# Off-diagonal blur products of a two-level pyramid issued as two 64-row tiles on TensorE

## The chip, the cores and the metric

One core of a Trainium2 chip runs the whole program once. The metric is the device time of that execution in microseconds. Beside it there is one profiled execution, whose trace is read below.

## What is computed

The reference adds four blocks in sequence to an input of 16 images, 64 channels and 16x16 pixels. Each block begins with a group norm. The change touches the second block, which needs a small blur pyramid of the normalised input:

```python
G = x; pyr = [x]
for i in range(2):
    G = depthwise_gauss(G, gauss2d(2*i + 3, 1.6 * 2**(i/3)))   # 3x3, then 5x5, zero padded
    pyr.append(G)
for i in (1, 2):
    L = pyr[i-1] - pyr[i]
    A = softmax(L, over pixels) @ L.T                           # 64x64 for each image
    att = att + softmax(A)
```

The other parts of this block (keys, queries, values, the attention of the level 0) run around it. The pixels of an image are called tokens here: 256 tokens, row by row.

## The kernel before

All arithmetic is fp32, and each fp32 matmul stands in the trace as two instructions. Images go in pairs, two images times 64 channels on the 128 partitions: 8 tiles `t` of 128 by 256, in two groups `g` of four, and in four pairs of tiles `j`. A hand-written order of steps, the list `SCHEDULE`, is walked by every engine, each doing its own share of each step. Around the change it reads: `add` (DVE: end of block 1), `pyramid` of group 0, `norm` 1 of group 1, `levels` 0, `in1` 0, `levels` 1, `in1` 1, `levels_T` 0, `pyramid` of group 1, `levels_T` 1, then `levels` of group 1 between the `scores1` of group 0. So PE issues the second group's mean product (`group_means`, L376) right behind the first pyramid, and the whole norm of group 1 waits for it: DVE L887 to L889, GpSimd's power L1587, DVE L897, and L905, which writes the normalised tiles.

A blur of a token-major tile is a product with a 256 by 256 matrix: `lap1` and `lap2` hold identity minus blur 1, and blur 1 minus blur 2. The input `xT` has the tokens on the partitions, in two chunks `k` of 128 tokens (NK = 2). For each level `s` and output chunk `jn`, `pyramid` claims a PSUM bank and accumulates two full 128x128 by 128x512 products, `k` = 0 and 1. ACT copies each bank to SBUF as `lT` (L1428, `pyramid_out`). The blur matrices are banded: an output token depends on tokens at most three image rows, 48 tokens and a few, away. So of the product with the other chunk only the 64 tokens next to the border between the chunks have weights that are not zero.

`claim` takes the next bank of a ring of six, and puts a wait on PE for the engine that last read that bank:

```python
n = ring[kind][claimed[kind] % len(ring[kind])]
if n in reader: pe.wait_ge(*reader[n])
reader[n] = (sem_of_reader, value)
```

The banks that the second pyramid takes are, six claims back, those of `xT`, keys, queries and values of the fourth pair (`in1` 1 of group 1). The bank of the keys is read last by ACT's exponentials of the keys, L1400 (`exp_keys`), which count `ek_ready`; L1400 itself waits for DVE's L1074. The queries' and values' banks are read by DVE L1093. In `in1`, ACT also does L1405 (copies of transposed banks), L1420 (exponentials of the levels) and L1434 (exponentials of the queries). Transposes on PE are L518, L554 (`level_back`), L565 (`exp_T`), L574 and L609; L521 and L528 are the projections; L589 are the channel products. After the second pyramid, DVE's L1085 (row maxima of a level) waits for L554.

Other places of the kernel already use parts of the array: `y2` (L457) runs two 64-row by 128-column tiles into two banks, `keys_values3` (L716, L718) four 64 by 64 tiles, next to full products (L658 ahead, L705 behind).

Of the kernel before, what the change touches and what calls it, by code (L numbers as in the profile page):

```python
# [27 lines left out]
NK = HW // P  # L28
# [104 lines left out]
def program(nc, x_in, const_in, weight_in, param_in, out):  # L133
# [11 lines left out]
    with ExitStack() as ctx:  # L145
# [8 lines left out]
        def bank(n, a=0, b=512):  # L154
            return psum[:, n * 512 + a:n * 512 + b]
# [8 lines left out]
        def cst(name):  # L164
            return const[:, const_at[name][0]:const_at[name][1]]
# [9 lines left out]
        lap = [None, cst("lap1").rearrange("p (k n) -> p k n", k=NK), cst("lap2").rearrange("p (k n) -> p k n", k=NK)]  # L175
# [56 lines left out]
        def tokens_of_pairs():  # L232
            return pairs(HW, "p (k t c) -> p k t c", 2, k=NK)
# [19 lines left out]
        xT = tokens_of_pairs()  # L253
        lT = [xT] + [tokens_of_pairs() for _ in range(2)]
# [98 lines left out]
        def claim(pe, key, sem_of_reader, value, kind="bulk"):  # L353

            n = ring[kind][claimed[kind] % len(ring[kind])]
            claimed[kind] += 1
            if n in reader:
                pe.wait_ge(*reader[n])
            reader[n] = (sem_of_reader, value)
            where[key] = n  # L360
            return n
# [5 lines left out]
        def _(pe):  # L367
            mm, tr = nc.tensor.matmul, nc.tensor.transpose
# [163 lines left out]
            def pyramid(g):  # L532

                pe.wait_ge(xT_ready, 2 * g + 2)
                for s in (1, 2):
                    for jn in range(NK):
                        step = (g * 2 + s - 1) * NK + jn
                        n = claim(pe, ("lT", step), lT_ready, step + 1)
                        for k in range(NK):
                            last = mm(bank(n), lap[s][:, k, jn * 128:(jn + 1) * 128],  # L540
                                      xT[:, k, 4 * g:4 * g + 4, :].rearrange("p t c -> p (t c)"),
                                      start=(k == 0), stop=(k == NK - 1))
                        last.then_inc(lT_mm, 1)

            def level_back(j, s):

# [257 lines left out]
            def start3():  # L804
# [3 lines left out]
            steps = {"norm": group_means, "ctx": context, "gate": gates, "taps": tap_sums, "conv": shift_taps,  # L808
                     "y1": y1, "y2": y2, "y3": y3, "mlp1": channel_mlp1,
                     "mlp2": channel_mlp2, "h4T": tokens4, "conv7": conv7, "add": add0, "in1": in1, "pyramid": pyramid,  # L810
                     "levels": levels1, "levels_T": levels_T, "scores1": scores1, "mix": mix1, "out1": out1, "own": own_rows,
                     "residual": residual, "parts": tap_parts, "sums": sums, "start3": start3}
# [7 lines left out]
            for w in range(NT + STEPS_MORE):  # L820
                t, r = divmod(w, 4)
# [1036 lines left out]
```

## Time and profile before

| | |
|---|---|
| median of 3 runs | 274.06 us (273.55 to 275.35) |
| profiled execution | 272.08 us |
| its span, first to last instruction | 270.3 us |
| PE, DVE, ACT, POOL busy | 79%, 68%, 50%, 13% |
| both pyramids (L540) on PE | 14.2 us, 32 instructions |

PE is the matrix engine, PEld its weight loads, which run beside it. DVE is VectorE, ACT ScalarE, POOL GpSimd. In a timeline a row gives the start, the time, engine, line, operation, and in brackets how long the engine had been idle and who released it. Instructions of one line that follow each other are merged into one row. A matmul's own time is longer than the distance to the next one, as they are pipelined: the distance between starts is what a stream pays.

### The profile page before, as it was taken

What the parts mean: (1) busy time and instruction counts of PE and PEld (TensorE: products, weight loads), DVE (VectorE), ACT (ScalarE), POOL (GpSimd) and SP (SyncE); (2) the same over time, 40 slices, a digit from 0 to 9 for tenths busy, and PEclk for the clock granted to TensorE, in tenths of its full rate; (3) what the DMA queues carried; (4) which work ended last, traced back from release to release, by engine and by line L of the source; (5) the groups of instructions that cost most, each with busy time, mean ns of one, the idle gap of its engine ahead of it and who ended that gap; (6) DMA issues with size and microseconds to landing.
All of it is one profiled execution on the core that took longest, in us unless ns stands there. A gap on an engine that the chain in (4) does not pass through costs nothing. (4 is left out here: it accounts for less than half of the span.)

```text
span 270.3 us, 6261 instructions
## 1 busy us (share of the span) xinstructions
PE 214.1 (79%) x2402; PEld 129.9 (48%) x2402; DVE 185.1 (68%) x521; ACT 136.2 (50%) x338; POOL 35.5 (13%) x64
## 2 busy tenths in 40 slices
PE   0376898755499877989589599699789959998974
PEld 0344674423375565677454133345544634464552
DVE  2464533457689599198877647865968597779892
ACT  1025268823255367889554233774367455634510
POOL 1833000000100100000010467203320010000000
PEclk9999799998599999999999999999979999999995
DMA  6930000000000000000000045351034004400001
GB/s 183 407 140 2 1 0 4 0 2 0 0 0 0 4 0 0 0 4 2 2 4 2 24 118 145 76 132 41 6 84 105 10 0 114 125 19 22 4 19 58
DMA packets 8685, 12.57 MB, mean 46 GB/s; under 512 B 1616, under 2 KB 7888, under 8 KB 8400
## 3 DMA queue, kind: packets, MB, share of 16 engines
q1 hardware_dynamic: 8048, 11.37, 14.5%
q10 hardware_dynamic: 608, 0.80, 1.0%
q8 instruction: 19, 0.31, 0.5%
q14 instruction: 10, 0.08, 0.1%
HBM read 4.93 MB, written 1.05 MB: 22 GB/s over the span
## 5 line engine op out<-in xcount | busy, mean ns | idle before, releaser
L1512 ACT ACTIVATE region<-psum 128x512 f32<-128x512 f32 x32 | 19.0, 594 | 22.3 <-PE psum L767 22.1
L1506 ACT ACTIVATE region<-region 128x512 f32<-128x512 f32 x32 | 20.1, 628 | 19.3 <-DVE region L1246 19.1
L1239 DVE TENSOR_REDUCE smax<-psum 128x8 f32<-128x512 f32 x32 | 21.9, 684 | 8.3 <-PE psum L757 8.1
L1587 POOL TENSOR_TENSOR small<-small 128x4 f32<-128x4 f32 x8 | 8.2, 1023 | 146.6 <-DVE small L889 146.6
L739 PE MATMUL psum<-region,w 128*32 128x512 f32 x160 | 21.8, 616 | 2.2 <-ACT v_pad L1491 2.1
L767 PEld LDWEIGHTS psum<-const,region 128*128 128x128 f32 x128 | 14.2, 144 | 17.7 <-ACT region L1506 9.0
L1246 DVE TENSOR_TENSOR region<-psum,smax 128x512 f32<-128x512 f32 x32 | 22.0, 687 | 0.6
L767 PE MATMUL psum<-const,region 128*128 128x128 f32 x128 | 21.0, 287 | 1.6 <-ACT region L1512 1.6
L785 PE MATMUL psum<-region 128*64 128x18 f32 x512 | 20.5, 213 | 0.7 <-ACT region L1512 0.7
L785 PEld LDWEIGHTS psum<-region 128*64 128x64 f32 x512 | 17.5, 137 | 6.1 <-issue 5.2
L376 PE MATMUL psum<-small,const 128*128 128x8 f32 x16 | 3.6, 296 | 15.2 <-DVE small L878 15.2
L1405 ACT ACTIVATE region<-psum 128x512 f32<-128x512 f32 x20 | 11.0, 623 | 8.8 <-PE psum L518 8.8
L540 PE MATMUL psum<-region,const 128*128 128x512 f32 x32 | 14.2, 597 | 0.0
L871 DVE BATCH_NORM_STATS2 small<-X 128x6 f32<-128x256 f32 x32 | 12.3, 419 | 2.8 <-ACT X L1376 1.4
L1233 DVE SCALAR_TENSOR_TENSOR xn_pad<-v_pad,small,xn_pad 128x256 f32<-128x256 f32 x32 | 13.8, 476 | 0.0
L376 PEld LDWEIGHTS psum<-small,const 128*128 128x128 f32 x16 | 3.0, 232 | 19.8 <-DVE small L878 18.4
L1444 ACT ACTIVATE region<-psum,small 128x64 f32<-128x64 f32 x24 | 9.4, 425 | 5.7 <-DVE small L1125 5.7
L757 PE MATMUL psum<-region 32*64 32x256 f32 x256 | 9.9, 418 | 1.8 <-DVE region L1246 1.2
L1531 ACT ACTIVATE region<-psum 128x512 f32<-128x512 f32 x12 | 6.2, 609 | 9.2 <-PE psum L669 9.2
L1635 POOL COPY region<-v_pad 128x256 f32<-128x256 f32 x16 | 5.8, 404 | 37.8 <-ACT v_pad L1491 37.8
L411 PE MATMUL psum<-region 128*32 128x256 f32 x96 | 8.6, 508 | 2.3 <-issue 2.3
L528 PEld LDWEIGHTS psum<-weight,region 128*128 128x128 f32 x64 | 8.3, 204 | 4.2 <-ACT region L1405 2.2
(180 smaller groups left out, 472.6 us busy)
## 6 DMA issues: line engine op xcount, KB each, us to landing
region<-v_pad SPq DMA_DIRECT2D x60, 80.0 KB, 2.1
weight<-weight_in SPq DMA_DIRECT2D x1, 1600.0 KB, 12.8
const<-const_in SPq DMA_DIRECT2D x1, 1170.0 KB, 9.6
X<-x SPq DMA_DIRECT2D x4, 256.0 KB, 5.4
out<-xn_pad SPq DMA_DIRECT2D x8, 128.0 KB, 1.7
weight<-weight_in SPq DMA_DIRECT2D x1, 918.0 KB, 6.8
region<-xn_pad SPq DMA_DIRECT2D x6, 76.5 KB, 2.4
region<-xn_pad ACTq DMA_DIRECT2D x6, 76.5 KB, 2.5
```

Source lines behind the costliest of these rows:

```text
L540: last = mm(bank(n), lap[s][:, k, jn * 128:(jn + 1) * 128], xT[:, k, 4 * g:4 * g + 4, :].rearrange("p t c -> p (t c)"), start=(k == 0), st ...
L739: last = mm(bank(n)[32 * c:32 * c + 32, :], w4[:, c % 2, dx, :], v4[:, j % 2, c, :, :, dx:dx + W], start=(dx == 0), stop=(dx == 4), tile_p ...
L757: last = mm(bank(banks[r], a2 * 256, a2 * 256 + 256)[64 * c:64 * c + 64, :], q3[rows, j % 2, a, :], km[rows, j % 2, a, :, :].rearrange("p ...
L767: last = tr(bank(n, q * 128, (q + 1) * 128), e3[:, w % NE, q * 128:(q + 1) * 128], ident)
L785: last = mm(dst[half, a2, 1 - b, h:h + 2, :].rearrange("p h e -> p (h e)"), e3T[:, w % NE, at + 64 * c:at + 64 * c + 64], va[:, 4 * t + 2 ...
L871: v.bn_stats(stats[l][:, t, :], X[:, t, :]).then_inc(dve_small, 1)
L1233: v.scalar_tensor_tensor(out=a, in0=win, scalar=pe_w[:, 5 * PE_ROWS + i:5 * PE_ROWS + i + 1], in1=prev, op0=ALU.mult, op1=ALU.add).then_in ...
L1239: v.tensor_reduce(smax[:, w, :], src, X_AXIS, ALU.max).then_inc(smax_ready, 1)
L1246: v.tensor_tensor(s_sub[:, w % NE, :].rearrange("p (h m) -> p h m", h=HEADS), src, smax[:, w, :].unsqueeze(2).broadcast_to([P, HEADS, AP_] ...
L1405: a.activation(dst[:, :, 2 * j:2 * j + 2, :].rearrange("p k t c -> p t k c"), bank(where[(*key, step)]).rearrange("p (t k c) -> p t k c", ...
L1506: a.activation(e3[:, u % NE, :], s_sub[:, u % NE, :], ACT.Exp, scale=HD ** -0.5).then_inc(e3_ready, 1)
L1512: a.activation(e3T[:, u % NE, :], bank(where[("e3T", u)]), ACT.Copy).then_inc(e3T_ready, 1)
```

## The change

In each level both banks are claimed first. Then come the two diagonal products (output chunk `jn` with input chunk `jn`) with all 128 rows, and then the two off-diagonal ones over 64 rows only: for `jn` = 0 partitions 0 to 63 of chunk 1, for `jn` = 1 partitions 64 to 127 of chunk 0. They have different row positions in the array and different banks.

```diff
                 pe.wait_ge(xT_ready, 2 * g + 2)
                 for s in (1, 2):
+                    steps_of = [(g * 2 + s - 1) * NK + jn for jn in range(NK)]
+                    banks = [claim(pe, ("lT", step), lT_ready, step + 1) for step in steps_of]
                     for jn in range(NK):
-                        step = (g * 2 + s - 1) * NK + jn
-                        n = claim(pe, ("lT", step), lT_ready, step + 1)
-                        for k in range(NK):
-                            last = mm(bank(n), lap[s][:, k, jn * 128:(jn + 1) * 128],
-                                      xT[:, k, 4 * g:4 * g + 4, :].rearrange("p t c -> p (t c)"),
-                                      start=(k == 0), stop=(k == NK - 1))
-                        last.then_inc(lT_mm, 1)
+                        mm(bank(banks[jn]), lap[s][:, jn, jn * 128:(jn + 1) * 128],
+                           xT[:, jn, 4 * g:4 * g + 4, :].rearrange("p t c -> p (t c)"), start=True, stop=False)
+                    for jn in range(NK):
+                        near = slice(64 * jn, 64 * jn + 64)
+                        mm(bank(banks[jn]), lap[s][near, 1 - jn, jn * 128:(jn + 1) * 128],
+                           xT[near, 1 - jn, 4 * g:4 * g + 4, :].rearrange("p t c -> p (t c)"), start=False, stop=True,
+                           tile_position=(64 * jn, 0)).then_inc(lT_mm, 1)
```

The other engines' steps and all waits on `lT_mm` are as before.

## Rows read from the trace of the kernel before

**Rows 1.** Timeline, PE: both pyramids, and what stands behind them

```profile
81.61 1.99 PE L436 MATMUL psum<-region,const 8*128 8x256 f32 x8
83.53 7.13 PE L540 MATMUL psum<-region,const 128*128 128x512 f32 x16
90.50 0.28 PE L376 MATMUL psum<-small,const 128*128 128x8 f32 x2
...
105.76 7.11 PE L540 MATMUL psum<-region,const 128*128 128x512 f32 x16
112.71 1.47 PE L565 MATMUL psum<-const,region 128*128 128x128 f32 x12
...
115.33 0.60 PE L609 MATMUL psum<-const,region 128*128 128x128 f32 x4
```

**Rows 2.** Timeline, DVE: the norm of group 1, and behind the second pyramid

```profile
88.66 0.36 DVE L878 BATCH_NORM_AGGREGATE small<-small 128x2 f32<-128x6 f32 x4
90.82 0.16 DVE L887 TENSOR_TENSOR small<-small,psum 128x4 f32<-128x4 f32 x1 [1.81 <-PE psum L376]
...
108.56 0.69 DVE L1104 TENSOR_TENSOR region<-region,small 128x512 f32<-128x512 f32 x1
115.10 0.69 DVE L1085 TENSOR_REDUCE small<-psum 128x2 f32<-128x512 f32 x1 [5.85 <-PE psum L554]
```

**Rows 3.** Busy time by stretch: engine, us (instructions), then the granted clock

```profile
92.70:109.25 16.55, 12.93 (x76) 9.30 (x77) 15.99 (x36) 10.57 (x37) 0.00 (x0) 1.00 0.00 0
98.10:102.87 4.77, 1.95 (x12) 1.13 (x11) 4.63 (x11) 3.28 (x11) 0.00 (x0) 1.00 0.00 0
109.25:115.10 5.85, 5.85 (x31) 3.85 (x30) 0.00 (x1) 5.25 (x11) 0.00 (x0) 1.00 0.00 0
```

**Rows 4.** Timeline, PEld: weight loads of the first pyramid, first and last

```profile
84.07 0.19 PEld L540 LDWEIGHTS psum<-region,const 128*128 128x128 f32 x1 [0.24 <-issue]
84.50 0.19 PEld L540 LDWEIGHTS psum<-region,const 128*128 128x128 f32 x1 [0.24 <-issue]
...
89.65 0.19 PEld L540 LDWEIGHTS psum<-region,const 128*128 128x128 f32 x1 [0.24 <-issue]
```

**Rows 5.** Timeline in short windows, PE: 64x128 tiles (L457), then full rows

```profile
39.35 0.49 PE L457 MATMUL psum<-region 64*128 64x256 f32 x2
...
39.67 0.60 PE L457 MATMUL psum<-region 64*128 64x256 f32 x4
...
39.88 0.60 PE L457 MATMUL psum<-region 64*128 64x256 f32 x4
...
40.10 0.38 PE L457 MATMUL psum<-region 64*128 64x256 f32 x2
40.41 0.40 PE L411 MATMUL psum<-region 128*32 128x256 f32 x1
```

**Rows 6.** Timeline in short windows, PE: full, 64x64 tiles, full

```profile
160.05 0.59 PE L658 MATMUL psum<-xn_pad,weight 128*128 128x512 f32 x1
160.57 0.64 PE L716 MATMUL psum<-region,weight 64*64 64x512 f32 x1
...
161.06 0.59 PE L716 MATMUL psum<-region,weight 64*64 64x512 f32 x1
...
161.59 0.70 PE L705 MATMUL psum<-region,weight 128*128 128x512 f32 x1
...
162.13 0.19 PEld L652 LDWEIGHTS psum<-X,const 128*128 128x128 f32 x1 [0.24 <-issue]
```

**Rows 7.** L540's own page: times of one, minimum, median, maximum

```profile
L540 PEld LDWEIGHTS psum<-region,const x32: 186/190/192, 83.5 to 111.9; 128*128 128x128 f32 x32
L540 PE MATMUL psum<-region,const x32: 590/592/697, 83.5 to 112.3; 128*128 128x512 f32 x32
```

**Rows 8.** Timeline, ACT, with the releases of DVE and PE it stands in

```profile
98.86 0.47 ACT L1400 ACTIVATE region<-psum,small 128x256 f32<-128x256 f32 x1
99.22 0.20 ACT L1400 ACTIVATION_READ_ACCUMULATOR region<-psum,small 128x1 f32 x1
...
106.45 0.47 ACT L1400 ACTIVATE region<-psum,small 128x256 f32<-128x256 f32 x1
106.81 0.20 ACT L1400 ACTIVATION_READ_ACCUMULATOR region<-psum,small 128x1 f32 x1
...
110.77 1.57 ACT L1428 ACTIVATE region<-psum 128x512 f32<-128x512 f32 x3
112.91 0.60 ACT L1428 ACTIVATE region<-psum 128x512 f32<-128x512 f32 x1 [0.56 <-PE psum L540]
113.41 2.06 ACT L1405 ACTIVATE region<-psum 128x512 f32<-128x512 f32 x4
116.03 0.47 ACT L1420 ACTIVATE region<-psum,small 128x256 f32<-128x256 f32 x1 [0.56 <-DVE small L1086]
```

**Rows 9.** Timeline, PE and PEld: a wait for L1400, here and in the second pyramid

```profile
99.56 0.63 PE L554 MATMUL psum<-const,region 128*128 128x128 f32 x4 [1.45 <-ACT region L1400]
...
107.13 0.19 PEld L540 LDWEIGHTS psum<-region,const 128*128 128x128 f32 x1 [0.24 <-ACT region L1400]
```

## The prediction

> **What bounds the kernel now.** I read the page's engine shares first and then, as they average over unlike stages, only the timelines of PE, DVE and ACT from the first pyramid to the scores. The first pyramid is 16 instructions from 83.53 to 90.50, with PE gap-free before it [rows 1]. Behind it in PE's queue is L376, whose inputs were ready when DVE ended its aggregate at 88.66 + 0.36 = 89.02; DVE then idled 1.81 us until L376 [rows 2]. So the first pyramid holds back the whole norm of group 1, by at most about 1.4 us: L376 could begin near 89.1 instead of 90.50. From 92.70 to 109.25 DVE is busy 15.99 of 16.55 us [rows 3]: everything there hangs on when DVE begins, and moves with it. The second pyramid starts at 105.76 and ends where L565 starts, 112.71 [rows 1]. DVE idles 5.85 us up to 115.10, PE is busy for the whole 5.85 us [rows 2, 3]: the second pyramid lies on the path outright. Later work waits on semaphores, with no clock time of its own, so I let a shift at 115 go through to the end at full size.
>
> **The products removed.** In a stream of full products the weight loads start 0.43 us apart (84.07, 84.50, ... 89.65: 5.58 us over 13 steps) and are hidden behind the matmuls [rows 4]. A pyramid is 16 such slots. The change turns 4 products of a level (8 instructions) into 2 full ones (4) and 2 of 64 rows (4). If the two of 64 rows run side by side they fill 2 slots. L457 shows this very shape with half the columns: two instructions start together at 39.35, two at 39.67, two at 39.88, two at 40.10 [rows 5], 0.215 us apart in the steady part, which is half of 0.43 for half of 512 columns. So 64-row tiles with different row positions and banks do overlap, pair by pair, first passes together and second passes together. A level goes from 8 to 6 slots, a pyramid from 16 to 12: 4 x 0.43 = 1.72 us less.
>
> **The changes of tile shape added.** Each level now goes from full to tiles and back. Where shapes change, the trace has gaps. Into tiles: L658 to L716 is 160.05 to 160.57, 0.52 instead of 0.43, so 0.09 [rows 6]; the first tile slot is 0.49 there (0.06 more, with a 64-column load of weights), and 0.32 instead of 0.215 for L457, so 0.10 more, with a 128-column load as here [rows 5]. Out of tiles: 0.53 from 161.06 to 161.59, so 0.10; 0.54 from 161.59 to the next weight load at 162.13, so 0.11 [rows 6]; L457 to L411 has 0.31 instead of 0.215, again 0.10 [rows 5]. I read it as a wait for the array and a load that is no longer hidden, and take c = 0.20 us for one change of shape, 0.19 in and 0.21 out, the nearest rows in shape. Two a level, 0.80 a pyramid; the last one out falls on L376 or L565. Bounds: 0 if these products see none of it; at most 0.35, if the array waits for a matmul's whole end (0.59 less 0.43) and the whole load of 0.19 is exposed [rows 7]. A pyramid is then shorter by 1.72 - 0.80 = 0.92 us.
>
> The Trainium skill (TensorEngine Tiling (Array Packing), Key Properties) says the same in general: changing the tiling mode, as against the tile, drains TensorE, and it names no price. It speaks against this change; the gaps of rows 5 and 6 agree with it. Going by that rule the sum keeps its 0.80; without it, it would be the rival of a free change below.
>
> **First pyramid.** Its four banks' former readers are all over by 83.5 (PE had no gap there), so the earlier claims cost nothing. It ends 0.92 us sooner, L376 starts at 89.58, above the 89.1 at which DVE would be late. DVE, POOL and all up to 105 move by 0.92. ACT copies both banks of level 2 back to back at the end instead of one; they are ready near 90.6, ahead of the transposes of level 2, the last step of a queue that had 0.91 us to spare in front of 93.5. Gain: 0.92 us.
>
> **The wait added in the second pyramid.** The second bank claimed is that of the keys of the last pair. Its reader is ACT L1400, whose last piece runs to 106.81 + 0.20 = 107.01 [rows 8]. Before, this bank was needed only after four slots, and the trace shows the weight load at 107.13 just behind that reader [rows 9]: it had fitted by a hair. Now PE waits for it ahead of the first product. What is queued behind it on PE is the whole pyramid, and behind that all of L565, L574, L554 for which DVE waits. An L1400 that ends at 99.22 + 0.20 = 99.42 lets a matmul start at 99.56 [rows 8, 9], 0.14 later. So the pyramid starts at 107.15 instead of 105.76: 1.39 us lost. Both times move together with DVE's chain, as L1400 waits for DVE's L1074, so the earlier gain does not shorten this. The banks of level 2 were read by DVE L1093, over by 107.1, and cost nothing.
>
> In the old time frame the second pyramid goes from 107.15 to 107.15 + 6.95 - 0.92 = 113.18, against 112.71: 0.47 later. L565 to L554 and DVE's L1085 come 0.47 later too. The cover to watch is ACT: both last copies (L1428) come together, so L1405 x4 starts about 1.06 later than 113.41 and ends its issue near 116.4; ACT's next, L1420, was held by DVE until 116.03 [rows 8], now 116.50. It just fits; if it did not, each tenth would count on the path.
>
> **The sum.** First pyramid -0.92, second -0.92, wait +1.39: -0.45 us. The profiled execution would go from 272.08 (span 270.3 and 1.8 around it) to 271.6; the median shown lies 2.0 above that execution, so 274.06 becomes 273.6 us.
>
> **Rivals.** In general, with c for one change of shape, the result is -(3.44 - 8c - 1.39) us.
>
> *Changes of shape are free* (c near 0). For it: in both places where I read gaps a semaphore wait stands on one of the instructions too, and it may be part of them. Against it: the gap shows at every border. The first pyramid gains only its limit of 1.4, the second 1.72 - 1.39 = 0.33: -1.7 us, 272.3. The Trainium skill (TensorE: Matmul & The Clock Gate, Measured speedup vs the span model) gives a packed group as one matmul and some 4 ns for each further tile, with no term for the border, and would end here.
>
> *The border and the wait outweigh the saved slots*: slower. One mechanism, PE time in the pyramids, decided at 8c = 2.05, c = 0.26. At the bound c = 0.35 it is +0.75, 274.8. For it: c is measured once for each direction and the load here has the full 128 columns. Against: no row has over 0.22.
>
> *The wait does not come*, as it would if L1400 were done before 105.8: -1.84, 272.2. Only against it: 107.01 is read directly, and it moves with what precedes the pyramid.
>
> *The tiles do not overlap* when they accumulate onto a full product's bank: no slot is saved, and the sum is 1.60 + 1.39 = +3.0, 277.1. L457 starts its accumulation in the tile, so this exact case is not in the trace; its overlap speaks against.
>
> *The clock falls* in the longer idle of PE. Against: from 98.10 to 102.87 PE is busy 1.95 of 4.77 us and the granted clock is 1.00 [rows 3]. At 1.2 GHz the second pyramid's 6 us could double at worst.
>
> **How the numbers follow.** The forecast has 0.53; free borders 0.13; outweighed 0.17; no wait 0.05; no overlap 0.04; clock 0.02; the rest, 0.06, lies on both sides. The forecast's own range, c from 0.15 to 0.25, is 273.2 to 274.0. The three runs of before span 1.8 us, so a median can lie most of 1 us off. The range goes from 272.0 (free borders, no wait) to 275.3 (c at its bound and half a us of scatter). A difference under 1%, 2.7 us, is about what a measurement of this kernel cannot tell from none. No rival that gains reaches it (the largest is 1.84), so faster has 0.04, from scatter; slower has the overlap, the clock and scatter on top of a larger c, 0.08.
>
> **What would show it.** In the profile after: the two 64-row instructions of a pass start within 0.01 us, and level by level slots of 0.43, then about 0.52, 0.53, 0.53, 0.54; L540 and its successors 12 slots and 6.05 us from start to successor; L376 near 89.6 and DVE idle near 0.9 before L887; PE idle about 1.4 before the second pyramid, put down to ACT L1400; DVE idle before L1085 about 6.3; the clock 1.00 throughout. A pyramid of 5.3 us means free borders; one above 6.35 us means that they outweigh; one above 7 that nothing overlaps; no gap before 105 means that I misread the bank ring.

## The result, and the profile after

The changed kernel takes 275.68 us (median of 20 runs, 273.63 to 281.02), the kernel before beside it 273.81 us (20 runs, 270.55 to 277.19). The medians are 1.87 us apart, 0.7%, where 0.45 us less was forecast, and 275.68 lies outside the stated range of 272.0 to 275.3. The ratio is 1.0097, 95% interval 1.0067 to 1.0127. The ratios, here and below, leave out executions more than 1.5% above the fastest of the same kernel, which are those above 274.6 us for the kernel before and those above 277.7 for the change, so they can overstate a loss that comes in some executions only. By either measure the change is slower, by 0.7 to 1%.

The pyramids themselves went nearly as forecast. PE's timeline after the change (start, time, engine, line):

```profile
79.83 1.99 PE L436 MATMUL psum<-region,const 8*128 8x256 f32 x8
81.75 1.98 PE L539 MATMUL psum<-region,const 128*128 128x512 f32 x4
83.67 1.13 PE L543 MATMUL psum<-region,const 64*128 64x512 f32 x4
84.72 1.98 PE L539 MATMUL psum<-region,const 128*128 128x512 f32 x4
86.64 1.13 PE L543 MATMUL psum<-region,const 64*128 64x512 f32 x4
87.70 0.39 PE L376 MATMUL psum<-small,const 128*128 128x8 f32 x2
...
104.44 1.96 PE L539 MATMUL psum<-region,const 128*128 128x512 f32 x4 [1.25 <-ACT region L1402]
106.33 1.13 PE L543 MATMUL psum<-region,const 64*128 64x512 f32 x4
107.39 1.99 PE L539 MATMUL psum<-region,const 128*128 128x512 f32 x4
109.31 1.13 PE L543 MATMUL psum<-region,const 64*128 64x512 f32 x4
110.36 1.53 PE L567 MATMUL psum<-const,region 128*128 128x128 f32 x12
...
128.28 1.08 PE L620 MATMUL psum<-region 64*64 64x256 f32 x8
```

L539 are the full products, L543 the tiles. The first pyramid takes 81.75 to 87.70, 5.95 us against 6.97 in [rows 1]. Four tile instructions take some 1.05 us up to the next full product, where two slots of 0.43 would be 0.86. PE (TensorE) now idles 1.25 us before the second pyramid, and the releaser is L1402, which is L1400 of before. That pyramid takes 5.92 us, against 6.95.

As the two executions differ ahead of the pyramids too, where the code is the same, I measure from an anchor: the start of the last L436 block before the first pyramid (81.61 in [rows 1], 79.83 here). To the start of the second block of out products of the first group (L618 before, at 130.56; L620 after, at 128.28) it is 48.95 us before and 48.45 after: 0.50 us gained. I call this the anchor distance, and that second block the anchor block. From there to the end of the span it is 270.3 - 130.56 = 139.7 before and 271.8 - 128.28 = 143.5 after: 3.8 us lost. And up to the anchor, where the two programs are the same, it was 1.78 us less. The sum, -1.78 - 0.50 + 3.82, is the +1.54 of the two spans.

DVE and ACT after, the rows that answer to [rows 2, 8]:

```profile
88.12 0.16 DVE L889 TENSOR_TENSOR small<-small,psum 128x4 f32<-128x4 f32 x1 [0.88 <-PE psum L376]
...
112.81 0.69 DVE L1087 TENSOR_REDUCE small<-psum 128x2 f32<-128x512 f32 x1 [6.26 <-PE psum L556]
```
```profile
110.46 1.09 ACT L1430 ACTIVATE region<-psum 128x512 f32<-128x512 f32 x2 [1.31 <-PE psum L543]
111.43 2.08 ACT L1407 ACTIVATE region<-psum 128x512 f32<-128x512 f32 x4
113.73 0.47 ACT L1422 ACTIVATE region<-psum,small 128x256 f32<-128x256 f32 x1 [0.21 <-DVE small L1088]
```

DVE's idle ahead of the norm fell from 1.81 to 0.88, the one behind the second pyramid grew from 5.85 to 6.26, and ACT still had 0.21 to spare.

Where the 3.8 us went is in the stretches behind 128 us. Busy time by stretch of the kernel before. A row gives the stretch, its length, the busy time of PE, PEld, DVE, ACT and POOL with the number of instructions, then the granted clock (1.00 is 2.4 GHz, 0.50 is 1.2 GHz), the busy share of the DMA engines and what they moved in GB/s:

```profile
64.96:75.20 10.24, 4.24 (x13) 3.10 (x14) 7.73 (x28) 1.88 (x2) 1.04 (x1) 0.50 0.00 0
...
131.65:134.39 2.74, 0.00 (x1) 0.00 (x1) 2.58 (x13) 2.43 (x12) 0.00 (x0) 1.00 0.00 0
134.40:151.90 17.50, 16.40 (x284) 8.38 (x284) 11.70 (x56) 7.88 (x23) 2.02 (x2) 1.00 0.01 2
151.98:155.01 3.03, 0.00 (x0) 0.00 (x0) 2.97 (x12) 0.84 (x2) 1.58 (x1) 1.00 0.11 25
155.10:198.10 43.00, 37.32 (x478) 18.45 (x478) 31.34 (x69) 22.98 (x40) 16.46 (x24) 1.00 0.33 83
```

and of the changed one:

```profile
63.10:73.30 10.20, 4.03 (x12) 2.91 (x13) 7.72 (x27) 1.88 (x2) 1.04 (x1) 0.50 0.00 0
73.40:129.30 55.90, 49.35 (x461) 34.40 (x460) 44.63 (x133) 38.44 (x123) 1.01 (x1) 1.00 0.01 1
129.36:131.40 2.04, 0.00 (x0) 0.00 (x0) 1.94 (x8) 2.00 (x11) 0.00 (x0) 0.99 0.00 0
131.40:138.20 6.80, 6.11 (x94) 5.42 (x110) 3.96 (x22) 2.29 (x10) 1.01 (x1) 0.50 0.00 0
138.30:155.20 16.90, 12.86 (x207) 5.15 (x175) 11.38 (x52) 7.07 (x18) 2.64 (x2) 1.00 0.03 6
155.30:158.70 3.40, 3.40 (x58) 1.64 (x63) 0.65 (x4) 0.00 (x0) 3.40 (x3) 0.50 0.84 244
```

Both kernels have an idle of PE of 2.74 us ahead of the third norm's L376 and one of 3.04 us ahead of the fourth's, in which PE waits for DVE's L878 (L880 after). Neither grew. PE before the change:

```profile
134.39 0.39 PE L376 MATMUL psum<-small,const 128*128 128x8 f32 x2 [2.74 <-DVE small L878]
...
135.19 2.09 PE L589 MATMUL psum<-region 128*64 128x64 f32 x64
...
155.01 0.39 PE L376 MATMUL psum<-small,const 128*128 128x8 f32 x2 [3.04 <-DVE small L878]
```

But in the changed kernel the clock fell at 131.4, within the first of them, and at 155.3, right behind the second:

```profile
132.09 0.59 PE L376 MATMUL psum<-small,const 128*128 128x8 f32 x2 [2.74 <-DVE small L880]
...
133.56 3.68 PE L591 MATMUL psum<-region 128*64 128x64 f32 x64
...
155.15 0.53 PE L376 MATMUL psum<-small,const 128*128 128x8 f32 x2 [3.04 <-DVE small L880]
```

L591 takes 3.68 us there; the same line, L589 of before, takes 2.09 at full clock. From this L376 to the fourth norm's it is 20.62 us before (134.39 to 155.01) and 23.06 after (132.09 to 155.15), 2.44 more; from that one to the next L652 block (L654 after) 3.67 before (155.01 to 158.68) and 5.07 after (155.15 to 160.22), 1.40 more. The two make up the 3.8.

So the question is why 0.5 us less work should make the clock fall at idles that were there all along. Theory "clock": the loss is those stretches and nothing else; its sharper form, theory "shift", says that the clock's fall depends on when an idle comes, and the change moved it. Rivals: the new wait ahead of the second pyramid causes it; or the loss lies in the pyramids' claims and tiles; or the changed mix of PE's work makes the clock fall, wherever the idles lie.

In what follows, the clock mean is the mean granted clock of a whole timed execution. It sums up how long the clock was down, but doesn't say where; that only the profiles tell, one for each kernel. Of 126 executions of the kernel before, in the five comparisons below, 63 had 0.947 or more; of the changed kernel's 32, none had.

### The profile page after: what moved, and what is told of

It is laid out like the page before. It is cut to its first block and busy times, and to the rows that moved or that the text cites. A ratio compares the mean times of both kernels' runs of the same rounds, so it can differ in the third digit from the quotient of the medians.

```text
span 271.8 us, 6263 instructions
## 1 busy us (share of the span) xinstructions
PE 217.3 (80%) x2402; PEld 131.2 (48%) x2402; DVE 185.1 (68%) x521; ACT 136.1 (50%) x338; POOL 35.4 (13%) x64
## 3 DMA queue, kind: packets, MB, share of 16 engines
HBM read 4.93 MB, written 1.05 MB: 22 GB/s over the span
## 5 line engine op out<-in xcount | busy, mean ns | idle before, releaser
L1514 ACT ACTIVATE region<-psum 128x512 f32<-128x512 f32 x32 | 19.0, 593 | 22.3 <-PE psum L769 22.1
L376 PE MATMUL psum<-small,const 128*128 128x8 f32 x16 | 4.1, 328 | 14.6 <-DVE small L880 14.6
L376 PEld LDWEIGHTS psum<-small,const 128*128 128x128 f32 x16 | 3.3, 260 | 19.5 <-DVE small L880 18.7
L671 PE MATMUL psum<-xn_pad,weight 32*32 32x512 f32 x216 | 11.4, 686 | 1.0 <-ACT region L1533 1.0
L591 PE MATMUL psum<-region 128*64 128x64 f32 x256 | 9.9, 246 | 0.5 <-ACT region L1446 0.5
```

Source lines behind the costliest of these rows:

```text
L591: last = mm(bank(n, s * C, (s + 1) * C)[half, :], left[:, k, half], right[:, k, half], start=(k == 0), stop=(k == NK - 1), tile_position=( ...
L671: last = mm(bank(banks[r])[32 * dy:32 * dy + 32, :], hetT[rows, 3 * dy + dx, :], xn_pad[rows, ts, dy:dy + W, dx:dx + W], start=(dx == 0), ...
L1514: a.activation(e3T[:, u % NE, :], bank(where[("e3T", u)]), ACT.Copy).then_inc(e3T_ready, 1)
```

## The experiments

### One part alone, and the idles filled

a1 claims both banks of a level first and keeps the products:

```diff
+banks = [claim(pe, ("lT", step), lT_ready, step + 1) for step in steps_of]
 for jn in range(NK):
-    n = claim(pe, ("lT", step), lT_ready, step + 1)
     for k in range(NK): ...full products as before...
```

> Both banks of a level claimed first, the products as before (8 full instructions a level). Anchor for all runs: from the start of the last L436 before the first pyramid to the start of the second block of out products of the first group (L618 in the kernel before) is 48.95 us before and 48.45 us with the change. Theory 'wait and slots' (the pyramid's own PE time is as predicted, and the rest of the loss is the clock later): the second pyramid starts 1.3 to 1.4 us later against what precedes it, the anchor distance is 50.3, the first pyramid keeps 6.97 us. Whole time: +1.4 us in executions whose clock is that of before. Rival 'claims are free' (the wait was hidden): anchor 48.95, time as before. Rival 'clock alone' says nothing of the anchor, but if any shift of the work moves the half-clock stretches, the time differs from +1.4 by several tenths to 3 us either way.

a2 is the change with the second claim moved behind the first full product:

```diff
-banks = [claim(...) for step in steps_of]
+banks = []
 for jn in range(NK):
+    banks.append(claim(pe, ("lT", steps_of[jn]), lT_ready, steps_of[jn] + 1))
     mm(bank(banks[jn]), ...full product...)
```

> The change, but the second bank of a level is claimed only ahead of its own full product. By the slots the wait for the keys' bank shrinks from 1.39 to 1.39 - 0.86 = 0.5 us: anchor distance 48.45 - 0.85 = 47.6 us, pyramids' own time 5.9 us each. If the claims carry the loss, this kernel is 0.85 us faster than the change and, by the anchor, 1.35 faster than before. If the clock carries it, the whole time lies wherever the half-clock stretches fall, and may still be above the kernel before; the profile would again show 0.50 clock around the idle of PE in front of the third norm's L376.

a3 and a4 add products to the kernel before and to the change, in `group_means`, ahead of its wait:

```diff
+filler = {(2, 0): 3, (3, 0): 3}.get((l, g), 0)
 ...the claim of the norm's own bank n comes ahead of the filling...
+for _ in range(filler):
+    mm(bank(n), ident, cst("spread"), start=True, stop=True)
 pe.wait_ge(gn_mv[g], NG * (l + 1))
```

> The kernel before, with three more full products (ident by a constant, result overwritten, 6 instructions, 2.6 us at full clock) placed in PE's idle of 2.74 us ahead of L376 of the third norm's first group, and three in its idle of 3.04 us ahead of L376 of the fourth norm's first group. They keep PE busy there. Theory 'clock': the runs of before are spread over 270.6 to 277.2 because some of them lose the clock at these two places; filled, the spread shrinks and the median comes down to the low end, 271 to 272.5, clock mean of a run 0.95 or more in nearly all. Rival 'not the clock': the products cost nothing or some tenths, and the median stays near 273.8 or above.

> The change, with the same added products at the same two places. Theory 'clock': the two half-clock stretches after 130 us (131.4 to 138.2 and 155.3 to 158.7 in the profile after) are gone, and what remains of the change is what the anchor shows, -0.5 us against the kernel before with the same filling; median near 271 to 272. Rival 'the loss is in the pyramids or in what they delay': this kernel stays 2 to 3 us slower than the filled kernel before.

Measured on one chip, with the kernel before at 272.49 us (25 runs):

| | median us (range, runs) | ratio to before | anchor distance | anchor block to end | clock mean 0.947 or more |
|---|---|---|---|---|---|
| a1 claims only | 278.15 (275.8 to 280.1, 6) | 1.0213 [1.0159, 1.0267] | 50.35 | 139.7 | 0 of 6 |
| a2 late claim | 275.21 (274.6 to 277.4, 6) | 1.0142 [1.0092, 1.0192] | 47.45 | 145.2 | 0 of 6 |
| a3 before, filled | 272.69 (270.6 to 273.9, 12) | 1.0020 [0.9985, 1.0055] | 48.87 | 139.8 | 11 of 12 |
| a4 change, filled | 271.62 (270.5 to 273.3, 12) | 0.9992 [0.9956, 1.0028] | 48.38 | 139.9 | 10 of 12 |

The anchor distances settle the local part: the claims cost 1.40 us (50.35 against 48.95, 1.4 expected), the late claim wins 1.5 (47.45, 47.6 expected). In the page of waits of a1 the wait is plain:

```profile
PE psum L540 <- ACT region L1400: 1.3, 1, 1.3
```

But a2, on that path 1.5 us shorter than the kernel before, has a median 2.7 us above it. Its stretches after the return of the clock at 76.1:

```profile
76.20:134.00 57.80, 49.46 (x461) 34.21 (x461) 46.81 (x141) 40.87 (x135) 1.01 (x1) 1.00 0.01 1
134.20:137.50 3.30, 3.30 (x56) 2.97 (x56) 2.07 (x9) 0.60 (x1) 1.01 (x1) 0.50 0.00 0
137.70:154.50 16.80, 13.84 (x228) 5.89 (x224) 11.48 (x53) 8.23 (x24) 1.52 (x2) 1.00 0.01 2
154.70:161.40 6.70, 5.82 (x82) 2.54 (x82) 3.21 (x14) 0.00 (x0) 5.32 (x4) 0.50 0.51 143
```

The fillings take the loss away. The change with 5 us of useless products in PE's idle has a median of 271.62, 0.9 us below the kernel before beside it, where without them it was 1.9 above: 2.7 us faster by doing more. In its timeline they stand in the idle (here L376 is the filling, and L382 is the mean product, L376 of the other kernels):

```profile
130.77 2.84 PE L376 MATMUL psum<-const 128*128 128x512 f32 x6
133.66 0.39 PE L382 MATMUL psum<-small,const 128*128 128x8 f32 x2
```

and from its stretch table, no fall from 74.5 to 221:

```profile
74.60:131.00 56.40, 49.84 (x465) 34.84 (x465) 45.36 (x133) 38.70 (x125) 1.01 (x1) 1.00 0.01 1
131.00:138.00 7.00, 6.95 (x121) 4.23 (x124) 5.10 (x24) 3.00 (x13) 1.01 (x1) 1.00 0.01 2
138.00:151.20 13.20, 12.10 (x176) 5.01 (x173) 9.13 (x45) 7.29 (x22) 1.01 (x1) 1.00 0.01 2
151.20:158.00 6.80, 6.46 (x93) 2.86 (x89) 3.79 (x18) 0.91 (x3) 5.29 (x3) 1.00 0.49 138
```

Filled, the changed kernel is below the filled kernel before, 271.62 against 272.69, where 0.5 was expected; the intervals of their ratios overlap, so the gain in time is not shown, only that the loss is gone. The filling of the kernel before narrowed its spread (270.4 to 276.9 became 270.6 to 273.9) and left its median alone, as half its executions had no loss to begin with. a3's median was to come down to 271 to 272.5, and did not. The larger miss: a1 was to be 1.4 us slower and is 5.7, with no execution at 0.947 or more, though its profile has the full clock from 80.1 to 202.8. That profile lost its time elsewhere: its anchor stands at 85.12 us, 3.5 later than in the kernel before, and up to the anchor the programs are the same; these 3.5 and the 1.4 of the claims make up the 4.9 us between the two spans. The mean of its three executions at a clock mean of 0.931 is 1.1 us above that of the three of the kernel before at 0.930, near the 1.4. Why a1's executions all had the low clock means is not shown.

### Which half, and the better form

b1 uses the new code for `g == 0` only, b2 for `g == 1` only. b3 is a2 with the fillings of a3. b4 is b3 with seven more products ahead of L491, L376 and L518 between 55 and 72 us.

> The change in the first pyramid only, the second as before. Anchor distance (start of the last L436 before the first pyramid to the start of the second block of out products of the first group): 48.95 - 1.0 = 47.95 us (what it was measured to be for the change, 6.97 to 5.95 us, all passed on by the norm of group 1). Theory 'clock later': the whole time is nevertheless not 1 us better than before; the runs at a clock of 0.95 or more are about 1 us faster than those of before, and the others lose 2 to 5 us to half-clock stretches behind 130 us. Rival 'the wait of the second pyramid is what makes PE idle and the clock fall': no such loss here, median 1 us below before.

> The change in the second pyramid only. Anchor distance 48.95 + 1.39 - 1.03 = 49.3 to 49.4 us. Rival 'the wait is the cause of the clock loss': this kernel shows the loss of the whole change, 2 to 3 us above before. Theory 'clock later, by where PE's idle of 2.7 and 3.0 us lies': 0.4 us above before at equal clock, and a loss that depends on the execution.

> The kernel with the late claim of the second bank, with three added products in PE's idle ahead of the third and of the fourth norm's first group, as in the filled kernels. Without them it had the shortest anchor distance (47.45 us, 1.5 below before) and yet took 275.2. Theory 'clock': anchor 47.4, median about 1 us below the filled change, 270.5 to 271, and below the kernel before. Rival: stays near 275.

> As the last one, and with further added products in PE's idle between 55 and 72 us (2 ahead of L491's first block, 2 ahead of L376 of the second norm's first group, 3 ahead of L518's first block), where every profile so far has a half-clock stretch of 10 us or more from about 65 on. Theory 'clock': that stretch shrinks or goes, and PE's L521, L528 and L501 behind it run at full clock: 1 to 3 us faster than the last one. Rival: PE in that stretch is not what sets the time, or the added products, if the clock has fallen already, are themselves late: same or slower.

| before: 273.3 (35 runs) | median us (range, runs) | ratio to before | anchor distance | clock mean 0.947 or more |
|---|---|---|---|---|
| b1 first only | 274.04 (271.1 to 277.5, 12) | 1.0077 [1.0039, 1.0115] | 48.04 | 1 of 12 |
| b2 second only | 273.57 (272.0 to 278.0, 12) | 1.0071 [1.0031, 1.0110] | 49.38 | 6 of 12 |
| b3 late, filled | 272.46 (269.4 to 274.2, 12) | 0.9998 [0.9954, 1.0043] | 47.53 | 9 of 12 |
| b4 late, all filled | 271.94 (270.4 to 272.8, 12) | 1.0012 [0.9984, 1.0041] | 47.45 | 8 of 12 |

b1 has no new wait and is 0.9 us shorter on the path, and it has the loss: its median is 0.7 us above the kernel before, and one execution in twelve had 0.947 or more. b2 has the wait and keeps that clock mean in half, as the kernel before does; its median is 0.3 above, where its path is 0.4 longer. (b2's one profile is of an execution that lost the clock.) So the wait ahead of the second pyramid is not the cause; that rival falls. b3 and b4 are no clear gain over the kernel before: b3's median was to be 270.5 to 271, and b4 was to be 1 to 3 us below b3. b4's seven products didn't remove the early half-clock stretch (59.2 to 72.9 in its profile) and saved nothing measurable. It does have the narrowest spread of the kernels with twelve executions or more.

### Which idle

c1 and c2 are a4 with only one of the two fillings, ahead of the third or of the fourth norm's L376; c3 is the kernel before filled at all places of b4; c4 is the change again.

> The change, with the three added products only ahead of L376 of the third norm's first group. The profile after had 6.8 us at half clock from 131.4, where channel products L591 took 3.68 instead of 2.08 us, and 3.4 us from 155.3. Theory 'clock, both places': this kernel gets back the larger part, 2 of the about 3.5 us between the change and its filled version, median 273 to 274, and the profile can still have a half-clock stretch about 155.

> The change, with the three added products only ahead of L376 of the fourth norm's first group. By the same theory it gets back the smaller part, about 1 to 1.5 us, median 274 to 275, and the profile can still have the stretch about 131. If one of the two places alone gives back all of the 3.5 us, the other has no part in it.

> The kernel before, filled at all places as in the late-claim kernel with all fillings. It gives the worth of the late-claim form of the change with the clock held on both sides: by the anchor distances (48.9 and 47.4) the late-claim kernel is 1.5 us faster than this one.

> The change itself once more, beside the partly filled versions on the same chip. By the clock theory its profile again has half-clock stretches behind 125 us that the kernel before lacks, near the idle ahead of the two L376, its anchor distance is 48.4 to 48.5 again, and its median is 2 to 3 us above before. If this execution keeps its clock there, its time is 0.5 us below an execution of before with the same clock mean.

| before: 273.22 (23 runs) | median us (range, runs) | ratio to before | clock mean 0.947 or more |
|---|---|---|---|
| c1 third norm filled | 275.72 (274.9 to 277.6, 6) | 1.0117 [1.0058, 1.0176] | 0 of 6 |
| c2 fourth norm filled | 275.01 (272.1 to 277.6, 12) | 1.0049 [1.0003, 1.0095] | 1 of 12 |
| c3 before, all filled | 272.93 (268.5 to 275.3, 12) | 0.9950 [0.9889, 1.0010] | 10 of 12 |
| c4 change again | 276.71 (274.2 to 280.7, 6) | 1.0102 [1.0018, 1.0187] | 0 of 6 |

The split that I expected, two thirds and one third, is wrong. c1, which was to give back the larger part, gives back nothing that its ratio shows. c2 may give back a part: its ratio is about half the change's, but the intervals overlap. Both fillings together, in a4, left no loss. c4, the change again, is 3.5 us above the kernel before, where 2 to 3 were expected. c1's profile has the full clock up to 151.9 and then half of it for 6.8 us, where the change's had 3.4; the stretch tables of c1, then c2:

```profile
131.00:151.90 20.90, 17.68 (x287) 8.59 (x285) 14.97 (x70) 9.62 (x31) 2.70 (x3) 1.00 0.01 2
152.10:158.70 6.60, 5.90 (x82) 2.53 (x82) 3.02 (x14) 0.00 (x0) 5.14 (x4) 0.50 0.51 145
```
```profile
133.30:139.90 6.60, 6.14 (x94) 5.41 (x110) 3.77 (x22) 2.05 (x9) 1.01 (x1) 0.50 0.01 2
140.10:177.50 37.40, 33.42 (x422) 13.52 (x398) 25.27 (x82) 16.86 (x36) 13.52 (x17) 1.00 0.25 66
```

The fall that c1 avoided brings its next idle forward, and the clock fell there too. This is a hint at the shift theory. Between b4 and c3 (271.94 and 272.93, in two comparisons on the same chip) lies 1.0 us of the 1.5 expected, and the scatter of either is as large.

Measured from the last return of the clock (64 to 80 us into the program) the profiles make a table. The idle ahead of the third norm's L376 begins so many microseconds behind that return:

| clock kept | clock fell, each time 58.0 behind the return |
|---|---|
| before 56.4, a1 56.6 | a2 54.7, c4 54.7, b1 55.6, b2 55.6, c2 55.8, the change 56.0 |

The change is 0.4 us on the wrong side. What puts an execution into one column is two things: the anchor distance, and how far ahead of the anchor the clock returned, which was 5.1 us in a1, b2 and c4 and 6.2 to 6.5 in the others. For the second idle it is alike, with a limit on either side: before (76.8) and a1 (76.9) kept the clock; a2, c1, c4 (76.3 to 76.4) lost it 78.5 behind the return, the change, b1 and b2 (78.6 to 78.8) 81.9 behind it.

### Useless work instead of idle

If it is the shift, the change must get faster by doing more. d1 and e2 put one useless product of half width into the second pyramid, e3 two, d2 four into the late-claim form, d3 one into the kernel before; e1 is the change.

```diff
 banks = [claim(...) for step in steps_of]
+for _ in range(1 if (g, s) == (1, 2) else 0):
+    mm(bank(banks[0], 0, 256), lap[s][:, 0, 0:128], xT[:, 0, 4:6, :]..., start=True, stop=True)
```

> The change, with one useless product of 128x128 by 128x256 (two instructions, 0.43 us) ahead of the second level of the second pyramid, whose result is overwritten. Anchor distance 48.45 + 0.43 = 48.9, that of the kernel before. In eight unfilled profiles the clock fell at the idle ahead of the third norm's L376 when that idle began 54.7 to 56.0 us behind the clock's last return (six of them), and did not when it began 56.4 or 56.5 us behind (the kernel before and the claims-only one). Theory 'shift': this kernel's executions are spread like those of before, 4 in 10 with a clock mean of 0.947 or more where the change had 0 in 26; median 273 to 274, so 1.5 to 3 us below the change although it does more. Rival 'mix of work': the change plus 0.4 us, 276, and none at 0.947 or more.

> The late-claim form with four such useless products (1.7 us) at the same place. Anchor distance 47.45 + 1.7 = 49.2, 0.2 above the kernel before. Theory 'shift': spread like before, 4 in 10 with a clock mean of 0.947 or more where the late-claim form had 0 in 6; median 273 to 274.5, below the 275.2 of the form without the useless work. Rival 'mix of work': 276.9.

> The kernel before, with one such useless product (0.43 us) at the same place. Anchor distance 49.4. By both theories it is 0.4 us above before at equal clock. By the shift theory the idle begins later, about 56.9 behind the clock's return in the executions that kept their clock, and nothing says that they should lose it: 4 in 10 or more at 0.947 or more. If even this loses the clock in all executions, every shift does, and the direction has no part in it.

> The change itself. Shift theory: none of its executions at a clock mean of 0.947 or more (0 of 26 so far), median 275.5 to 276.7, anchor distance 48.4 to 48.5.

> The change with one useless product (0.43 us). Shift theory: faster than the change alone on the same chip by 0.5 to 2 us, anchor 48.9. Rival 'mix of work': slower than it by 0.4 us.

> The change with two useless products (0.86 us). Anchor 49.3, the idle ahead of the third norm's L376 begins 57.3 behind the clock's return where the return is 6.9 ahead of the anchor, and 55.5 where it is 5.1 ahead, by the other profiles. Shift theory: no fall at that idle in the former executions, so some at 0.947 or more, and the median is below the change's in spite of 0.86 us more work. Rival: 0.9 us slower than the change.

| | median us (range, runs) | ratio to before | anchor distance | clock mean 0.947 or more |
|---|---|---|---|---|
| d1 change + 0.43 | 274.80 (273.5 to 276.5, 6) | 1.0102 [1.0050, 1.0153] | 48.89 | 0 of 6 |
| d2 late claim + 1.7 | 274.01 (272.0 to 281.5, 12) | 1.0046 [1.0014, 1.0079] | 49.17 | 7 of 12 |
| d3 before + 0.43 | 273.58 (270.9 to 280.2, 9) | 1.0042 [0.9995, 1.0088] | 49.31 | 5 of 9 |
| e1 change | 274.49 (274.1 to 276.1, 6) | 1.0106 [1.0051, 1.0161] | 48.36 | 0 of 6 |
| e2 change + 0.43 | 273.58 (271.7 to 276.9, 12) | 1.0041 [0.9990, 1.0093] | 48.81 | 6 of 12 |
| e3 change + 0.86 | 272.53 (271.4 to 280.2, 12) | 1.0021 [0.9977, 1.0064] | 49.32 | 9 of 12 |

The kernel before took 272.94 us (20 runs) beside the d kernels, and 273.42 (23 runs) beside the e kernels. Two expectations failed. d1's median was to be 273 to 274 us with 4 in 10 executions at 0.947 or more, and it had none; d1 alone would have spoken against the shift in its timed executions. e1 was to be 275.5 to 276.7 and is 274.49. (e3's idle was expected 57.3 us behind the return for a return 6.9 ahead of the anchor; it returned 6.35 ahead, and the idle began at 56.8, as the same sum gives.) On one chip, e1 to e3, the order is the one it demands: 274.49, 273.58, 272.53, each with 0.43 us more to do than the one ahead of it. The intervals of the ratios of e1 and e3 overlap by a little. The counts don't depend on them: of the change's 32 executions none had 0.947 or more, with one useless product (d1 and e2) 6 of 18 had, and with two (e3) 9 of 12. d2 has 7 of 12 where a2 had none of 6. The rival of the mix of work asked for none there, and for times that grow with the work; it falls. In d3 the kernel before keeps its clock mean in 5 of 9 although it is shifted, so not every shift loses the clock.

The stretches of e1 behind the return of its clock at 75.7, and then those of e3, whose clock returned at 76.4, with the idle ahead of L376:

```profile
75.80:133.70 57.90, 49.02 (x459) 33.96 (x457) 46.35 (x137) 40.67 (x134) 1.02 (x1) 1.00 0.01 1
133.90:140.50 6.60, 6.30 (x94) 5.42 (x110) 3.76 (x22) 1.98 (x9) 1.01 (x1) 0.50 0.01 2
```
```profile
76.50:133.00 56.50, 49.94 (x464) 34.94 (x462) 44.29 (x130) 38.48 (x123) 1.02 (x1) 1.00 0.01 1
133.10:140.00 6.90, 4.16 (x113) 3.29 (x112) 5.03 (x24) 3.03 (x13) 1.01 (x1) 1.00 0.00 0
140.00:158.20 18.20, 14.06 (x237) 6.16 (x232) 12.80 (x62) 8.12 (x24) 4.30 (x2) 1.00 0.11 29
158.40:161.60 3.20, 3.20 (x48) 1.24 (x24) 1.71 (x5) 0.02 (x1) 2.55 (x4) 0.50 0.46 130
```
```profile
135.86 0.39 PE L376 MATMUL psum<-small,const 128*128 128x8 f32 x2 [2.75 <-DVE small L882]
```

The table of the third norm's idle grows to 14 profiles without one exception: kept with d1 56.8, d2 56.4, d3 56.8, e2 56.7, e3 56.8; fell with e1, 55.6, again at 58.0. The other half of the evidence is the price: from the anchor block to the end it takes 139.6 to 139.8 us in the seven profiles that kept the clock there, and 143.5 to 145.2 in the seven that lost it. The timed executions have no profile; that they sort as the profiles do is inferred from their clock means. In d1, d3, e2 and e3 the second idle begins at 77.1 or 77.2, and the clock falls 81.9 behind the return for 3.4 us; in place of that the profile of before has one from 198.1 to 201.5, and the time from the anchor block to the end is the same, 139.6 to 139.7 us. d2 kept the clock at both idles (56.4 and 76.8).

## Why the prediction was wrong

**The pyramid's slots: right.** Twelve slots, the tiles' two passes side by side. The length was 5.95 and 5.92 us, 6.05 forecast; 1.03 off the old length instead of 0.92. Slots and borders read from L457 and from L658, L716, L705 [rows 5, 6] held for this shape and for a product that accumulates onto a full one. The rivals of free borders, of borders that outweigh the slots and of tiles that don't overlap are refuted. (The length at which borders and wait would outweigh the slots is 6.26 us by the sum of the prediction, 6.95 less half of 1.39, and not the 6.35 given there; both are far from 5.9.) The four borders of a pyramid cost some 0.7 us (1.72 less 1.03), not 0.80: the last one's share of 0.1 falls on the line behind. The first pyramid's surplus did not arrive, as the L376 behind it takes 0.39 instead of 0.28: DVE gained 0.92, as forecast.

**The wait: right.** The start of the second pyramid moved by 1.39 against what precedes it (24.61 from the anchor, against 24.15 less the 0.93 by which the L565 ahead of it came sooner), 1.39 forecast; a1 shows the claims' price by itself, 1.40.

**Everything up to 130 us: right.** -0.50 us by the anchor distance, -0.45 forecast, with the idle times of DVE (0.88, 6.26; forecast 0.9, 6.3) and ACT's cover, which just held. This is one profile of each kernel, and the seven others with the pyramids of the change or of the kernel before agree with them to 0.1 us (48.36 to 48.47, and 48.87 to 48.97).

**The step that failed** is the sentence that later work has no clock time of its own, so that a shift at 115 goes through to the end at full size. TensorE's clock has one, as these profiles show it: 56.4 us behind its return an idle of 2.7 us left it up, 56.0 us behind it did not. The kernel has idles of 2.7 and 3.0 us ahead of two norms, and whether the clock falls at them turned on when they came, to within 0.4 us. By their clock means about half the executions of the kernel before lay inside the good places; a shift of half a microsecond took the changed one out. I put this term at nothing, and it was 3.8 us in the profile after. I did list a fall of the clock, but only in the new idle ahead of the second pyramid, where it never fell in any profile, and with a chance of 0.02. The row that I held against it, 98.10 to 102.87 at full clock, has idles of PE of 1.45 and 1.38 us with work between them; it says nothing of an idle of 2.7 us elsewhere. The warning was in the runs of before: an execution spread of 1.8 us, 273.55 to 275.35, in a program with one core and no load besides, and a page whose clock line shows four stretches below full.

**The size.** At equal clock mean the change does about what the path says. Beside e1, four executions of the change at 0.936 or 0.937 took 274.14 to 274.69, five of the kernel before at 0.936 took 274.53 to 276.01; the means are 274.3 and 275.1. In c4 the same means are 0.3 us apart. So the 1.9 us between the measured medians can be read as 0.3 to 0.8 us gained and, as the remainder, two to three lost at the idles; this split is an estimate, as no timed execution shows where its clock was down.

**What stays open.** Why the clock's falls came at the same distances behind its last return, and why it returned 5.1 us ahead of the anchor in three profiles and 6.2 to 6.9 in eleven, no run tells. With 5.1 us, an estimate from the anchor distances puts the third norm's idle of the kernel before at 55.1 behind the return, among those where the clock fell; this would explain the executions that it lost, but no profile of the kernel before caught one. Why a1's timed executions were all at 0.942 or less is not shown either.

## What to carry to other kernels

Look at each idle of PE of the size of those here, 2.7 and 3.0 us, behind which PE work is on the path, and ask what it costs if the clock falls there; a change that moves such an idle by tenths of a microsecond can cost more than it saves, and one profile of each kernel doesn't tell. Compare executions by their clock mean, or fill the idles in both kernels, before judging a change of a microsecond. Claim a ring's banks as late as the first use allows: the early claim alone cost 1.4 us here.

## What the runs showed of the hardware

A change between full products and row tiles costs about 0.2 us: L539 to L543 starts 0.52 apart, the first tile slot is 0.53, the way back 0.52 and 0.53, against 0.43 in a stream. The weight load of the first tile starts with its matmul, at 83.66, 0.5 us behind the start of the matmul ahead, and that matmul takes 0.70 us instead of 0.60; I read half of the 0.2 as the load that is no longer hidden. From the timeline in short windows:

```profile
83.14 0.59 PE L539 MATMUL psum<-region,const 128*128 128x512 f32 x1
83.67 0.70 PE L543 MATMUL psum<-region,const 64*128 64x512 f32 x2
84.20 0.60 PE L543 MATMUL psum<-region,const 64*128 64x512 f32 x2
84.72 0.70 PE L539 MATMUL psum<-region,const 128*128 128x512 f32 x1
```

The Trainium skill (TensorEngine Tiling (Array Packing), Key Properties) says that a change of tiling mode drains TensorE. The gaps at all four borders agree with it, though they don't show that a drain makes them.

The clock fell 58.0 us behind its return in seven profiles out of seven that had the third norm's idle begin 54.7 to 56.0 behind it, and in none of seven with a begin at 56.4 to 56.8, for idles of the same 2.7 to 2.8 us. The Trainium skill (TensorE: Matmul & The Clock Gate, Part 1) says that the gate runs on its own time and does not start anew with a kernel. The profiles agree: with the same program up to there, the first half-clock stretch begins at 30.8 us in the kernel before and at 22.1 in the changed one. What the clock decided here is 0.7% between the medians of two kernels, and most of the 2.4% between the fastest and the slowest of 25 executions of the same one (270.4 to 276.9 us, beside a1 to a4).
